# Additive attention layer: later places for the probability copies, the weighted sum and the block's finish, and fills in pairs

## The reference

```python
hp = h @ lin_w.T + lin_b                      # [b, 1024, 64]
u, v = hp @ W1.T, hp @ W2.T
s = u[:, :, None, :] + v[:, None, :, :]       # [b, i, j, 64]
s = where(s > 0, s, 0.2 * s)
e = einsum('bijf,f->bij', s, a)               # one score for each pair of nodes
e = where(adj > 0, e, NEG_INF)
out = elu(softmax(e, axis=2) @ hp)
```

## Time and profile before

| | before |
|---|---|
| median of 3 runs | 3523.88 us |
| lowest and highest | 3518.64 and 3524.6 us |
| profiled execution, its own time | 3535.45 us |
| its span | 3533.6 us |
| additive layer, first score product to last exponentials | about 1270 to 3164 us |
| DVE, ACT, PE busy in the span | 86%, 82%, 87% |
| granted TensorE clock, mean of the span | 0.954 of full speed |

### The profile page before, as it was taken

The page is one execution under the profiler, slowest core; times in us unless marked ns, Lnnn a source line. Parts: engine busy times, 40 slices in busy tenths (PEclk is TensorE's granted clock), DMA queues, the critical chain, the costliest instruction groups (busy, mean ns, idle before and its releaser), DMA issues. The chain is left out here.

```text
span 3533.6 us, 78782 instructions
## 1 busy us (share of the span) xinstructions
PE 3074.6 (87%) x30972; PEld 1704.5 (48%) x30972; DVE 3034.8 (86%) x4698; ACT 2898.4 (82%) x3774; POOL 992.2 (28%) x869
## 2 busy tenths in 40 slices
PE   7988998999999879898898998988988888878875
PEld 5765666666666633333343333333333333336664
DVE  7886887878888789999999999999999999965775
ACT  4546887778877769999999999999999999975665
POOL 4434666666666600000000000000000000005674
PEclk9998999999999989999999999999999999987897
DMA  7640000000000000000000000000000000002221
GB/s 246 222 139 16 20 21 20 23 18 24 21 21 19 13 11 10 10 10 10 10 10 10 10 10 10 10 10 10 10 10 10 10 10 10 10 5 67 57 63 30
DMA packets 68411, 111.58 MB, mean 32 GB/s; under 512 B 26452, under 2 KB 26582, under 8 KB 68054
## 3 DMA queue, kind: packets, MB, share of 16 engines
q1 hardware_dynamic: 68054, 106.69, 9.8%
HBM read 86.61 MB, written 18.87 MB: 30 GB/s over the span
## 5 line engine op out<-in xcount | busy, mean ns | idle before, releaser
L1120 ACT ACTIVATE l_scalar_ring<-l_w,l_r 128x1024 f32<-128x1024 f32 x1568 | 1650.0, 1148 | 34.4 <-DVE l_values L1171 27.7
L1236 DVE TENSOR_SCALAR l_vector_ring<-l_w_code,l_r_code 128x2048 f32<-128x2048 f32 x1264 | 1605.9, 1341 | 3.1 <-PE scores L1045 0.5
L1035 PE MATMUL scores<-l_scalar_ring,l_signs 128*32 128x512 f32 x6272 | 767.9, 608 | 130.2 <-ACT l_scalar_ring L1120 129.9
L1045 PE MATMUL scores<-l_vector_ring,l_signs_code 128*32 128x512 f16 x10112 | 685.0, 396 | 90.4 <-DVE l_vector_ring L1236 89.6
L462 POOL TENSOR_TENSOR l_masked<-l_relu,mask 128x512 f32<-128x512 f32 x512 | 585.9, 1166 | 344.2 <-ACT l_relu L664 322.9
L250 ACT COPY probs_t<-turned 128x512 f32<-128x512 f32 x576 | 324.7, 587 | 430.1 <-PE turned L209 429.7
L172 POOL TENSOR_TENSOR stat<-stat,minus_half 128x8 f32<-128x8 f32 x32 | 71.6, 2239 | 1931.1 <-DVE stat L167 1931.0
L1045 PEld LDWEIGHTS scores<-l_vector_ring,l_signs_code 128*32 128x32 bf16 x10112 | 257.9, 96 | 543.2 <-DVE l_vector_ring L1236 213.8
L209 PE MATMUL turned<-ident,l_probs 128*128 128x128 f32 x3072 | 438.1, 288 | 12.2 <-issue 7.6
L277 ACT ACTIVATE l_probs<-l_logits,negmax 128x1024 f32<-128x1024 f32 x384 | 442.9, 1153 | 7.0 <-DVE negmax L268 7.0
L1035 PEld LDWEIGHTS scores<-l_scalar_ring,l_signs 128*32 128x32 f32 x6272 | 192.2, 110 | 492.3 <-issue 255.9
(11 more groups left out here) (249 smaller groups left out, 2857.6 us busy)
## 6 DMA issues: line engine op xcount, KB each, us to landing
mask<-masks_kept SPq DMA_DIRECT2D x192, 256.0 KB, 2.7
l_adj<-adj SPq DMA_DIRECT2D x64, 512.0 KB, 5.9
masks_kept<-l_mask_ring SPq DMA_DIRECT2D x64, 256.0 KB, 4.9
x_res<-x SPq DMA_DIRECT2D x8, 256.0 KB, 4.8
out<-x_res SPq DMA_DIRECT2D x8, 256.0 KB, 2.9
l_h<-l_h SPq DMA_DIRECT2D x8, 128.0 KB, 2.8
l_kl<-l_dh SPq DMA_DIRECT2D x32, 2.0 KB, 1.9
l_kl<-l_dl SPq DMA_DIRECT2D x32, 2.0 KB, 1.8
```

What stands on the lines that cost most here:

```text
L1035: last = nc.tensor.matmul(s.scores[g * ROWS:(g + 1) * ROWS, buf, half, :], signs[:, window], scalar_ring[:, at % SCALAR_RING, g, halves[ha ...
L1045: last = nc.tensor.matmul(s.scores[g * ROWS:(g + 1) * ROWS, buf, half, :], signs_code[:, par, g % 2, window], parts(vector_ring[:, at % VE ...
L1120: last = nc.scalar.activation(scalar_ring[:, at % SCALAR_RING, g, :], w[:, par, :], ACT.Relu, bias=r[:, par, column:column + 1])
L1236: last = nc.vector.tensor_scalar(vector_ring[:, at % VECTOR_RING, g:g + 2, :], w_code[:, par, :, :], r_code[:, par, 0, column:column + 1], ...
```

## The change

The change touches only the additive layer.

```diff
-        MAX, EXP, TURN, COPY, MULTIPLY, FINISH = 3, 6, 7, 10, 11, 15
-        BATCH, ELU = 1, 4
-        FILL_AT = {3: 0, 7: 1, 11: 2}
-        TAKE_AT = {k + 3: i for k, i in FILL_AT.items()}
-        FILLS = {1: 0, 2: 3, 3: 6}
+        MAX, EXP, TURN, COPY, MULTIPLY, FINISH = 3, 6, 8, 13, 14, 4
+        BATCH, ELU = 7, 11
+        FILL_AT = {1: 0, 9: 1}
+        TAKE_AT = {k + 6: i for k, i in FILL_AT.items()}
 
         def fills_of(n, project):
 
-            return (FILLS[n], 3) if project and n in FILLS else (0, 0)
+            return (2 * (n - 1), min(2, K - 2 * (n - 1))) if project and 1 <= n <= 5 else (0, 0)
...
-                    if n == 1 and k == 8 and b > 0:
+                    if n == 2 and k == 2 and b > 0:
                         elu_add(b - 1)
                     if encode and n == 4 and k == 5:
-                        v.wait_ge(sems["fill_copied"], (b + 1) * K + K)
+                        v.wait_ge(sems["fill_copied"], (b + 1) * K + 6)
                         extreme(0, w[:, 1 - par, :])
                     if encode and n == 5 and k == 3:
+                        v.wait_ge(sems["fill_copied"], (b + 1) * K + 8)
                         extreme(1, r[:, 1 - par, :])
...
+                    if k == FINISH and u > 1:
+                        finish((n - 2) % NB, buf, u - 2)
                     if k == BATCH and n == 1 and b > 0:
                         batch_end(b - 1)
                     if not before:
                         continue
                     if k == MAX:
                         logit(1 - buf, u - 1)
-                    if k == FINISH:
-                        finish((n - 1) % NB, 1 - buf, u - 1)
...
             logit(1, u)
+            finish(NB - 2, 0, u - 1)
             finish(NB - 1, 1, u)
```

## The result

| | before | changed |
|---|---|---|
| median | 3521.3 us (3517.1 to 3524.6, 4 runs) | 3469.3 us (3465.9 to 3471.9, 4 runs) |
| profiled execution | 3535.5 us | 3465.9 us |
| one graph, mean of graphs 1 to 6 | 237.55 us | 229.82 us |
| additive layer, start of the first products to start of the last exponentials | 1893.4 us | 1836.6 us |

A forecast was written before the change was run, and what follows sets the result against it. Waits between three engines were taken to bound the additive layer, with DVE's stream the next bound. Seven graphs at 5.2 us (36.4) plus 4 us in the last made about 40 us, from 3523.9 to 3483.5 us, range 3466 to 3510.

The forecast's parts named there:

- The floor: Additive layer: DVE's stream without waits needs 230.3 us per graph, so 7.2 us is all that can be won.
- The rests: DVE waits left per graph: 0.3 us in block 7, 0.7 in blocks 5 and 6, 1.0 for the lower clock.
- The clock's term: Stretches at PE's lower clock (1.2 GHz) make PE late for DVE's logits; 1.0 us per graph left for them.
- the last one: The last graph, without encoding: ACT sets its end, and 4 us of ACT's slack is taken as gain.
- COPY and TURN: ACT's probability copies moved from 10 to 13, transposes 7 to 8: margin at the next set turns from -0.2 to +2.3 us.
- FINISH: DVE's finish moved from set 15 to set 4, 20 sets on: its 38.3 us of waits over six graphs disappear.
- MAX is what is late next: DVE's reading of the scores for the logits, unmoved, becomes the next late place, with 0.2 us of margin in block 7.
- The fills: Fills in pairs, six sets between product and copy: ACT's 4.4 us per graph of waits vanish, costed at nothing afterwards.
- ELU, new waits of DVE on fills, tail: ELU steps and DVE's waits on 6 and 8 fills cost nothing; the tail's extra finish of 0.45 us is hidden.
- B: Half is given back at MAX: 4.6 us of rests per graph, gain 20 us, time 3504; chance 0.23.
- D: Weighted sum between sets 14 and 15 delays the scores by 1.9 us: slower, 3542 to 3588 at most; chance 0.06.
- this rule: Optimise the busiest engine first: DVE loses no work, so the additive layer would stay at its time; 3517 to 3531, chance 0.07.

The follow-up runs named there:

- act_48: The changed kernel with one set of block 6 moved from ACT to DVE: 3478.1 us, ratio to before 0.9875.
- max_2: The changed kernel with MAX at 2 instead of 3, so DVE asks for the scores one set sooner: 3483.5 us, ratio to before 0.9878.
- old_copy: The changed kernel with TURN, COPY and MULTIPLY back at 7, 10 and 11: 3496.1 us, ratio to before 0.991.
- finish_only: The kernel before with only the finish moved to set 4 of the block behind, with the ELU steps that follow it: 3488.9 us, ratio 0.9892.
- old_fills: The changed kernel with the fills of before, three in each of blocks 1 to 3: 3469.4 us, ratio to before 0.9835.
- pool_norm: The changed kernel with the additive layer's layer norm centring, squares and scaling on POOL instead of DVE: 3487.3 us, ratio to before 0.9879.
- copy_only: The kernel before with only TURN, COPY and MULTIPLY moved to 8, 13 and 14, the finish staying at 15: 3638.4 us, ratio 1.0305.

## Why the prediction was right, and where it was off

**The floor.** I had put DVE's stream at 230.3 us per graph and 7.2 us as all that could be won. The graph went to 229.8, 7.7 us less. DVE's waits went entirely; the rest is 0.5 us, nearly all of it in DVE's busy time (it was busy for 227.7 us and is for 227.3). act_48 and max_2 show that DVE is the bound: each adds its 2.5 and 2.4 us in full.

**The rests, the term that was mis-sized.** I left DVE 2.0 us of waits per graph, 0.3 in block 7, 0.7 in blocks 5 and 6 and 1.0 for the lower clock. All three are 0. For block 7 I had made it 0.3 us short, from a margin of 0.2 and a set that came 0.5 later; measured are 0.3 to 0.4 us to spare in blocks 6 and 7. The mechanism was right, but that the sign came out in the kernel's favour is no merit of the forecast. The later copy gave ACT the lead that kept the margin: without it, in old_copy, DVE waits 3.1 us per graph.

The clock's term took the low stretches as given. For the kernel before it was read rightly: a low stretch of 6.8 to 10.2 us stands behind the middle of block 5 in graphs 1, 2, 4 and 6, and just these have a wait at the logits in block 6, of 1.5, 0.2, 1.5 and 1.6 us. But the stretches didn't stay. The mean granted clock of the six graphs rose from 0.97 to 1.00, PE was busy for 1249.4 us instead of 1264.7, and the time at 1.2 GHz fell from 75 to 14 us: one stretch of 3.4 us in block 6 of four graphs, which cost DVE no wait.

Seven graphs gave 54.0 us instead of 36.4, and the last one 2.8 instead of 4, so the layer of the profiled executions gave 16.4 us more than forecast. The medians gave 52 us, 12 more. Why they gave less than the layer, no run shows, for the other executions have no trace.

**COPY and TURN.** The margin at the set behind the copy was to turn from -0.2 to +2.3 us. ACT's copy waits fell from 36.6 to 15.8 us, 2.6 per graph where I had left about 5, and no wait of PE for ACT is left in blocks 3 and 4. Counted out by set, PE's waits for scalar set 11 fell from 76.6 to 11.0 us in the six graphs; at set 14, where there were none, 17.3 us now stand, as said. 45.8 of the 48.7 us of PE's waits for ACT lie in blocks 5 and 6. Taken back, the part costs 3.2 us per graph.

**FINISH.** Right, with its mechanism: 5.1 us of the 7.7 come with it alone, and MAX is what is late next. That the ring of 4 would hold DVE too, as in finish_only and old_copy, I had not seen.

**The fills.** Right that their waits vanish and cost nothing in the changed kernel (old_fills: the same 1378.9 us); wrong as a statement on the kernel before, where they are worth 3.05 us per graph alone. The parts don't add: 5.1 for the finish, 3.05 for the fills and -15.1 for the copies alone would make -7.0, and together they gave 7.7. The copies lose only while the finish stands at 15, right behind the weighted sum; and the fills gain only while DVE has waits that they can shorten, since nothing goes below DVE's floor.

**ELU, new waits of DVE on fills, tail.** None of them shows a wait, as said. ACT's slack is 3.3 us instead of 5.3, because the period is shorter. The last graph gave 2.8 us, I had taken 4.

**The rivals.** B, waits given back at MAX, is what finish_only, old_copy and max_2 show at 2.3 to 3.1 us; the change avoids it by 0.3 us. D's picture was right too: the weighted sum does stand between ACT's late set 14 and the end of the scores, and the lag stayed just inside the margin. The section of the Trainium skill that names the busiest engine pointed at the right engine ("Perfetto Trace Analysis", "Identifying the Most-Contended Engine"), and what was to be had were the waits of that engine, not its work. That the layer would stay at its time by this rule was my own reading; the rule names the engine and doesn't say that its work must shrink.

## What to carry to other kernels

When three engines are busy for 88 to 96% of a period and none fills it, take the longest stream without its waits as the floor, and place each step so that the engine of that stream never waits. For each hand-over count how many finished pieces lie between the two places: a wait goes when the work between them is longer than the chain behind the hand-over, and a step must move together with the one that waits for it (the copies moved alone cost 15 us per graph, with the finish they gave 2.6). Where the margin left is 0.3 us, as at the logits here, say so in the code, since moving that place by one set of 2.5 us cost 2.4 us per graph.

## What the runs showed of the hardware

- POOL and DVE hinder each other: beside each POOL operation on 128x512 f32 tiles one DVE instruction took 0.7 us longer (in pool_norm four set instructions 6.56 us instead of 5.11 beside two of them, a coding step 1.27 us instead of 0.54). POOL's operations took 1.9 to 2.1 us there, and the same lines took 1.04 us in the other layers. An idle POOL was no free place for DVE's work.
- TensorE's granted clock changed with the order of the work alone: in six graphs with the same work the time at the lower level (1.2 GHz) fell from 75 us before to 14 after, while PE's waits for the other two fell from 160 to 127 us. The sum of the waits doesn't decide it: in copy_only PE waits for 251 us in six graphs, and 27 us are at the lower level.
- The stretch from the layer's last exponentials to the end took from 352.1 to 373.1 us from one profiled execution to another, and in the 14 executions its length went with the time at the lower level, from 112 to 166 us (correlation 0.97). PE was busy for 252 us in the shortest and 275 in the longest, with 2109 products in both. What sets that time from one execution to the next stays open. A change of 8 us in one layer is therefore better read in that layer's own period than in the total.
